# Third expert layer: the shared expert's eight tiles from normed rows on chip, with the routing interleaved

## The reference

```
gelu = lambda t: jax.nn.gelu(t, approximate=False)
shared = gelu(x @ W1s + b1s) @ W2s + b2s
rw = jax.nn.softmax(x @ Wr, axis=-1)
topw, topi = jax.lax.top_k(rw, 2)
topw = topw / jnp.sum(topw, axis=-1, keepdims=True)
mask = jnp.sum(jax.nn.one_hot(topi, 8) * topw[..., None], axis=-2)
h = gelu(jnp.einsum('bsd,edf->bsef', x, W1p) + b1p)
priv = jnp.einsum('bsef,efd->bsed', h, W2p) + b2p
return shared + jnp.einsum('bsed,bse->bsd', priv, mask)
```

## Time and profile before

| | us |
|---|---|
| median of three runs | 1201.09 (1198.06 to 1204.16) |
| profiled execution | 1190.06 |
| its span, first to last instruction | 1188.3 |
| TensorE busy | 951.9 (80%) |
| VectorE busy | 737.2 (62%) |
| ScalarE busy | 504.8 (42%) |
| GpSimd busy | 468.1 (39%) |
| mean granted TensorE clock | 0.891 |

### The profile page before, as it was taken

How to read it: one execution, slowest core, us unless ns; L and a number is a source line. 1 busy time by engine, 2 the same in 40 slices (tenths; PEclk the granted TensorE clock), 3 DMA queues, 4 the chain that set the end, 5 groups by cost and what they waited for, 6 DMA issues and landing times. The chain is left out here.

```text
span 1188.3 us, 23797 instructions
## 1 busy us (share of the span) xinstructions
PE 951.9 (80%) x7426; PEld 885.7 (75%) x7426; DVE 737.2 (62%) x1699; ACT 504.8 (42%) x933; POOL 468.1 (39%) x480
## 2 busy tenths in 40 slices
PE   5784978528888859856995999999628995899993
PEld 1684878525888859855895999999625885899993
DVE  4586655475777757647555656665454786666664
ACT  2151656310555617631102777776413451343441
POOL 1052565211867626530132355554103452345441
PEclk9695999869879969997997999999859997899997
DMA  6005965410000053744124051119440003846853
GB/s 231 1 23 174 299 222 175 123 41 0 6 10 10 10 182 99 229 137 130 54 67 177 29 196 35 37 47 334 175 128 2 6 14 114 312 162 206 278 186 125
DMA packets 65388, 142.22 MB, mean 120 GB/s; under 512 B 11008, under 2 KB 42656, under 8 KB 60320
## 3 DMA queue, kind: packets, MB, share of 16 engines
q1 hardware_dynamic: 55520, 114.52, 28.3%
q0 software_dynamic: 9792, 26.75, 7.5%
HBM read 219.36 MB, written 18.61 MB: 200 GB/s over the span
## 5 line engine op out<-in xcount | busy, mean ns | idle before, releaser
L1602 PE MATMUL r_pH<-e_xsT,e_w 128*128 128x128 f32 x2560 | 309.0, 278 | 25.5 <-DMA e_w<-w_in 20.6
L1602 PEld LDWEIGHTS r_pH<-e_xsT,e_w 128*128 128x128 f32 x2560 | 298.4, 194 | 29.5 <-issue 22.5
L1551 POOL DMA_INDIRECT y_rows<-e_ys,e_to x102 | 166.5, 1632 | 259.6 <-DVE e_idx L1670 122.2
L1682 DVE TENSOR_TENSOR e_w_lo<-e_w,e_w_hi 128x1024 fp32r<-128x1024 f32 (+1 forms) x102 | 156.2, 1532 | 45.8 <-ACT e_w_hi L1638 45.1
L1615 PE MATMUL r_pY<-e_w_hi,e_h_hi 128*128 128x256 f32 x528 | 159.1, 301 | 7.4 <-issue 5.8
L1638 ACT ACTIVATE e_w_hi<-e_w 128x1024 fp32r<-128x1024 f32 (+1 forms) x102 | 132.3, 1297 | 70.3 <-DMA e_w<-w_in 70.2
L1687 DVE TENSOR_TENSOR e_h_lo<-xnT,e_h_hi 128x512 fp32r<-128x512 f32 (+1 forms) x102 | 86.6, 849 | 119.8 <-ACT e_h_hi L1654 119.8
L1615 PE MATMUL r_pY<-e_w_lo,e_h_hi 128*128 128x256 f32 x528 | 150.4, 285 | 0.0
L1615 PE MATMUL r_pY<-e_w_hi,e_h_lo 128*128 128x256 f32 x528 | 150.4, 285 | 0.0
L448 PE MATMUL g_o<-g_V,g_pT 128*128 128x65 f32 (+2 forms) x896 | 145.0, 319 | 4.8 <-ACT g_pT L407 4.8
L1650 ACT ACTIVATE xnT<-r_pH,e_w 128x128 f32<-128x128 f32 x416 | 115.5, 377 | 71.3 <-PE r_pH L1602 71.1
(11 more groups left out here) (275 smaller groups left out, 1412.9 us busy)
## 6 DMA issues: line engine op xcount, KB each, us to landing
e_w<-w_in SPq DMA_DIRECT2D x64, 1024.0 KB
e_w<-w_in SPq DMA_DIRECT2D x84, 512.0 KB
e_w<-w_in SPq DMA_DIRECT2D x32, 1028.0 KB
e_w<-w_in SPq DMA_DIRECT2D x52, 514.0 KB
e_b<-b_in SPq DMA_DIRECT2D x84, 128.0 KB
e_w<-y_rows SPq DMA_DIRECT2D x24, 256.0 KB, 5.0
p_adj<-adj_in SPq DMA_DIRECT2D x8, 512.0 KB, 7.4
xn_rows<-xn SPq DMA_DIRECT2D x32, 128.0 KB, 1.7
```

The lines of the kernel that those rows point to most:

```text
L1551: pool.indirect_dma_start(out=y_rows[:, :], in_=ys[b][:, :], in_offset=None, out_offset=bass.IndirectOffsetOnAxis(ap=to[b][:, :], axis=0))\
L1602: ins = nc.tensor.matmul(pH[b % 2][:, f, :], w1[b][:, at:at + P], xsT[b % 2][:, c, :], start=(c == 0), stop=(c == DC - 1))
L1682: nc.vector.tensor_tensor(w2_lo[b % 2][:, :], w2[b][:, :], w2_hi[b % 2][:, :].bitcast(F32), ALU.subtract).then_inc(w2_split, 1)
```

## The change

The shared expert's weights get buffers of their own for the whole kernel (w1_own, w2_own, b2_own) and are loaded during graph2, behind the second adjacency tile in SyncE's queue. A class OwnTiles computes the eight shared tiles ahead of the loop: `rise` reads the turned normed rows xnT directly, so that no rows are loaded, turned or copied; w2's rounding and remainder are made once; `end` adds the result to x at once, so that nothing of it goes through y_rows. The steps of `gate` are cut into parts that each engine issues between the steps of these tiles: TensorE counts ranks behind the first `rise` and makes the table of pairs behind the fourth `fall`; VectorE has slots at k = 0, tiles at 1, columns at 2, rows and destinations at 5; ScalarE its column at 2. Their results in PSUM move from pH to pT. The 72 matmuls of `rouse` go in this layer. The routed tiles are then tiles 0 to 21 of the loop, with HEAD = 2 turns written out; their slots' first guess is expert 0 and expert 4. The eighth shared `fall` and `end` are queued behind the first routed `rise`. `combine` loads and adds two rows. hT gets buffers of its own in this layer, since xnT stays in use. The other layers keep their order.

```diff
...
+        w1_own, w2_own = keep("w1_own", [P, DC * 1024 + 1024 // P]), keep("w2_own", [P, 1024 // P * D])
+        b2_own = keep("b2_own", [P, D])
         lg = keep("lg", [P, NT, 16])
...
+                            for buf, src in own_weights:
+                                sp.dma_start(buf, src).then_inc(own_loaded, 16)
                     front.store(sp)
...
+
+            def tensor_table(pe):
...
-                rouse(spare, 72)
-
-            def scalar_part(act):
+                if spare is not None:
+                    rouse(spare, 72)
...
+            links = []
+
+            def vector_onehots(dve):
+                links.append(linker(dve, vd))
+                link = links[0]
...
-                if shared:
-                    nc.vector.tensor_copy(dest[:, 0:first], own[:, 0:first])
-                    nc.vector.memset(etab[0:1, 0:first], E)
-
+
+            def vector_slots(dve):
+                link = links[0]
...
+            def vector_tiles(dve):
+                link = links[0]
...
+
+            def vector_columns(dve):
+                link = links[0]
...
+                nc.vector.tensor_scalar(etab[0:1, 0:R], et[:, :], float(E - 1), None, ALU.min)
+                nc.vector.tensor_scalar(more[:, :], turns[0:1, :], float(-HEAD), None, ALU.add).then_inc(tiles_known, 1)
+
+            def vector_rows(dve):
+                link = links[0]
...
-            K = 3 if shared else 2
...
+            K = 2
...
-                    if shared:
-                        link(nc.vector.tensor_tensor(acc, acc, yg[t][:, 2, :], ALU.add))
...
+        class OwnTiles:
...
+            def rise(self, pe, k):
+                F = self.FC * P
+                if k == 0:
+                    pe.wait_ge(self.loaded, 48)
+                if k >= 2:
+                    pe.wait_ge(self.ready, k - 1)
+                for f in range(self.FC):
+                    for c in range(DC):
+                        ins = nc.tensor.matmul(self.pH[k % 2][:, f, :], w1_own[:, c * F + f * P:c * F + (f + 1) * P],
+                                               xnT[:, c, k * P:(k + 1) * P], start=(c == 0), stop=(c == DC - 1))
+                ins.then_inc(self.risen, 1)
+            def fall(self, pe, k):
+                pe.wait_ge(self.w_split, 1)
+                pe.wait_ge(self.split, k + 1)
+                if k >= 2:
+                    pe.wait_ge(self.kept, k - 1)
+                m = k % 2
+                for f in range(self.FC):
+                    for n, (h, w) in enumerate(((self.h_hi, self.w2_hi), (self.h_hi, self.w2_lo), (self.h_lo, self.w2_hi))):
+                        ins = nc.tensor.matmul(self.pY[m][:, :], h[m][:, f, :], w[:, f * D:(f + 1) * D],
+                                               start=(f == 0 and n == 0), stop=(f == self.FC - 1 and n == 2))
+                ins.then_inc(self.fallen, 1)
+            def clear(self, pe, b):
+                if b == 1:
+                    pe.wait_ge(self.ready, NT)
+            def round_weights(self, act):
+                act.wait_ge(self.loaded, 48)
+                nc.scalar.activation(self.w2_hi[:, :], w2_own[:, :], ACT.Copy).then_inc(self.w_rounded, 1)
+            def activate(self, act, k):
+                F, m = self.FC * P, k % 2
+                act.wait_ge(self.risen, k + 1)
+                if k >= 2:
+                    act.wait_ge(self.split, k - 1)
+                    act.wait_ge(self.fallen, k - 1)
+                for f in range(self.FC):
+                    ins = nc.scalar.activation(self.hT[m][:, f, :], self.pH[m][:, f, :], self.function,
+                                               bias=w1_own[:, DC * F + f:DC * F + f + 1])
+                ins.then_inc(self.ready, 1)
+                act.wait_ge(self.ready, k + 1)
+                nc.scalar.activation(self.h_hi[m][:, :, :], self.hT[m], ACT.Copy).then_inc(self.rounded, 1)
+            def split_weights(self, dve):
+                dve.wait_ge(self.w_rounded, 1)
+                nc.vector.tensor_tensor(self.w2_lo[:, :], w2_own[:, :], self.w2_hi[:, :].bitcast(F32), ALU.subtract)\
+                    .then_inc(self.w_split, 1)
+            def split_hidden(self, dve, k):
+                m = k % 2
+                dve.wait_ge(self.rounded, k + 1)
+                nc.vector.tensor_tensor(self.h_lo[m][:, :, :], self.hT[m], self.h_hi[m][:, :, :].bitcast(F32), ALU.subtract)\
+                    .then_inc(self.split, 1)
+            def end(self, dve, k):
+                m = k % 2
+                dve.wait_ge(self.fallen, k + 1)
+                nc.vector.tensor_tensor(self.ys[m][:, :], self.pY[m][:, :], b2_own[:, :], ALU.add).then_inc(self.kept, 1)
+                dve.wait_ge(self.kept, k + 1)
+                nc.vector.tensor_tensor(x[:, k, :], x[:, k, :], self.ys[m][:, :], ALU.add)
...
-                hT = [xnT[:, n, 0:F].rearrange("p (f q) -> p f q", q=P) for n in range(2)]
+                if own_loaded:
+                    hT = [ph.sb(f"hT{n}", [P, FC, P])[:, :, :] for n in range(2)]
+                else:
+                    hT = [xnT[:, n, 0:F].rearrange("p (f q) -> p f q", q=P) for n in range(2)]
...
-                        return E if shared else b * E // UN
+                        return b * E // UN
...
-                        if isinstance(i, int) and t < first:
-                            if not early(i, b, UN):
-                                pool.wait_ge(turned, t - UN + 1)
-                            pool.dma_start(xs[b][:, :], xn_rows[t * P:(t + 1) * P, :]).then_inc(xs_loaded[b], 16)
-                            return
                         if not early(i, b, UN):
                             pool.wait_ge(turned, t - UN + 1)
-                        pool.wait_ge(idx_ready, t - first + 1)
+                        pool.wait_ge(idx_ready, t + 1)
                         pool.nop(nofuse=True)
...
+                        if own and early(i, b, UN):
+                            pe.wait_ge(own.kept, NT - 1 + b)
...
                     def step(i, b):
                         turn(i, b)
+                        if own and early(i, b, UN):
+                            own.clear(pe, b)
                         if not early(i, b, 1):
                             rise(*before(i, b, 1))
+                        if own and early(i, b, 2) and b == 1:
+                            own.fall(pe, NT - 1)
                         if not early(i, b, 2):
                             fall(*before(i, b, 2))
-                    gate_tensor(pe)
+                    ranks, table_of_pairs = gate_tensor
+                    if own:
+                        for k in range(NT):
+                            own.rise(pe, k)
+                            if k == 0:
+                                ranks(pe)
+                            if k > 0:
+                                own.fall(pe, k - 1)
+                            if k == 4:
+                                table_of_pairs(pe)
+                    else:
+                        ranks(pe)
+                        table_of_pairs(pe)
                     last = loop(pe, step)
                     rise(last, UN - 1)
                     fall(last, UN - 2)
...
+                        if own and early(i, b, UN):
+                            act.wait_ge(own.fallen, NT - 1 + b)
+                            act.wait_ge(own.split, NT - 1 + b)
...
-                    gate_scalar(act)
+                    exps, column = gate_scalar
+                    exps(act)
+                    if own:
+                        own.round_weights(act)
+                        for k in range(NT):
+                            own.activate(act, k)
+                            if k == 2:
+                                column(act)
+                    else:
+                        column(act)
...
-                        if not early(i, b, first - UN):
-                            next_rows(b, t + UN - first)
+                        next_rows(b, t + UN)
...
+                        if own and early(i, b, 2) and b == 1:
+                            own.end(dve, NT - 1)
...
-                    gate_vector(dve)
-                    dve.wait_ge(rows_known, 1)
-                    if not shared:
+
+                    def first_rows(dve):
+                        dve.wait_ge(rows_known, 1)
                         for b in range(UN):
                             next_rows(b, b)
-                    gate_dest(dve)
+                    onehots, slots, tiles, columns, rows, destinations = gate_vector
+                    onehots(dve)
+                    if own:
+                        for k in range(NT):
+                            for part in {0: [slots, own.split_weights], 1: [tiles], 2: [columns],
+                                         5: [rows, first_rows, destinations]}.get(k, []):
+                                part(dve)
+                            own.split_hidden(dve, k)
+                            if k > 0:
```

(6 more changed lines are left out.)

## The result

The changed kernel takes 1181.01 us, the median of four runs (1178.82 to 1184.53); the kernel before, timed beside it, takes 1199.80 (1198.06 to 1204.16). The ratio is 0.9849, with a 95% interval of 0.9819 to 0.9879, or 18.1 us less. The profiled execution took 1179.99 us, 10.1 less than that of before, at a mean granted clock of 0.894. So the change makes the kernel faster, by a little more than the forecast 15.3 us; the forecast time was 1185.8 us, and the measured 1181.01 lies at the lower edge of its own range, 1181 to 1192. In three later comparisons, each on a chip of its own, the kernel before took 1190.69 to 1191.55 us, so only ratios and savings are compared across comparisons.

What follows compares the result with a forecast made beforehand. Routing was taken as bound by VectorE's chain, the tiles by TensorE; 10.1 us saved at the layer's start plus 5.2 at its end, 15.3 off the median 1201.09, gives 1185.8 us, own range 1181 to 1192, all cases 1178 to 1196.

Steps and rivals of the forecast that it cites:

- First product and slow clock: At the layer's start, first product 3.49 us plus 1.7 lost to the low clock, bounds 0 and 3.5.
- Ranks: TensorE's rank matmuls, placed behind the first own product at the layer's start, would take 1.3 us.
- Stall before the first second product: TensorE would wait 1.5 us for VectorE's slots and two splits before tile 0's product 2, bounds 0 and 3.
- No wait between: Routing pieces between shared tiles stay hidden, 1.7 us of slack left; rival that they are not covered: about 1194, chance 0.12.
- Handover: From shared to routed tiles, first routed product 3.9 us after the seventh second product, a stall of 3.5.
- the loop's count: VectorE's reading of the count before copying the turned routed rows, taken as 0.7 us, bounds 0.2 and 1.5.
- To the first routed product: From the third expert layer's start to its first routed product, 57.7 us against 69.0, 11.3 saved.
- Clock at the handover: A clock fall after the wait before the first routed product, charged 1.2 us, bounds 0 and 3.
- End of the layer: Combining two rows instead of three cuts 19.62 us after the last add to 14.45: 5.2 saved, bounds 4 and 6.
- Own weights: Their 2.2 MB of loads in SyncE's queue of the graph stage would cost 0, bounds 0 and 2.
- GpSimd beside VectorE: Six slot comparisons, 3.57 us, beside VectorE's split of the weights, would cost nothing.
- The rival price: GpSimd comparisons of 0.6 us before each split make the first second product's stall 2.7 us, time 1187.0; no chance given.

Runs made afterwards that it cites:

- e6: Changed kernel with a third row per tile loaded and added into an unread buffer when combining: 1181.60 us, ratio 0.9911 to the kernel before.
- e9: Changed kernel with no edit, timed again: 1174.92 us against 1191.15 for the kernel before, ratio 0.9874.
- e3: Changed kernel with the first two routed tiles turned before the last own first product and copied earlier: 1171.72 us, ratio 0.9835 to the kernel before.
- e5: Changed kernel with routing pieces slots, tiles and columns all ahead of VectorE's split of the own weights: 1185.65 us, ratio 0.9939 to the kernel before.
- e4: Changed kernel with 42 idle-filling matmuls around the last steps of graph2, before the layer's entry: 1173.27 us, ratio 0.9831 to the kernel before.
- e7: Changed kernel with both the early turns and copies and the 42 filling matmuls before the layer's entry: 1169.65 us, ratio 0.9797 to the kernel before.
- e1: Changed kernel with the routing and its 72 filling matmuls back in one piece ahead of the shared tiles: 1189.22 us, ratio 0.9993 to the kernel before.
- e10: Early turns and copies plus 42 filling matmuls on the changed kernel, run again beside the unedited changed kernel: 1167.27 us, ratio 0.9805 to the kernel before.
- e2: Kernel before with two rows combined, the shared expert's row neither loaded nor added (output incomplete): 1188.77 us, ratio 0.9987 to the kernel before.

## Why the prediction was right

The forecast saved 15.3 us. The layer's distances, each the mean of the two profiles of a kernel, give 244.3 - 229.1 = 15.2, and the two timings 18.1 and 15.0. That the layer agrees to 0.1 us is partly luck: the start gave 11.2 (11.3 forecast), the end 4.1 instead of 5.2, and the 1.2 charged for a fall of the clock at the handover weren't paid in either profile of the changed kernel, so that two mis-sized terms cancel. The forecast time of 1185.8 started from the 1201.09 of the first timing, and is 4.8 us too high: 1.3 by the kernel before, whose median came out at 1199.80 beside the changed one, and the rest by the saving. The steps, in the prediction's order:

- **First product and slow clock: undersized.** I gave the low clock 1.7 us. From its start to the ranks it took 5.81, so 2.3 were lost; it took 5.1 in e6, 6.2 in e9, 6.3 in e3 and 6.5 in e5, a loss of 1.6 to 3.0, and with the fillers 3.6 (e4, e7). The low stretch that I took for the price, lasted 3.4 us; here the clock was low in all of the first 3 us and about half of the next. The bound of 3.5 held.
- **Ranks 1.1 (1.3 forecast), table 0.5 (0.7).** Both a little cheaper.
- **Stall before the first second product: 1.5, as forecast.** The order of events, ranks, slots, two splits, was the forecast one: the second product came 6.14 us after the first product's end instead of 6.3. The forecast counts from start to start (1.11 for the ranks, 3.49 for the product, then 1.54 of stall); the 1.21 in the row's bracket is shorter because the last matmul's modelled end, 3.82 after the product's start, lies later.
- **No wait between.** VectorE's pieces stay under TensorE's work as worked out, and e5 shows the other case: with the pieces in one lump 9.4 us come back. The 1.7 us of slack in the prediction are those of the hidden rows' way to the second product; what a piece has to fit in is VectorE's idle time of a tile, 4.42 us.
- **Handover: 2.86 of idle time (3.5), the mechanism shown by e3.** From the end of the seventh second product, 687.39, the first routed product came after 3.47 us, not 3.9. The oversized term is the loop's count, which no row had priced: VectorE's idle time before the copy is 0.24 us, and 0.7 was assumed. (That the 0.24 us are the reading of the count is argued from the program's order; the row names no releaser.)
- **To the first routed product: 57.7 forecast, 57.66 measured, 58.03 again.** The exact agreement is partly luck: the clock's 0.6 us and some 0.1 of small differences too few, and the handover's 0.4 and the small steps' 0.4 too many, cancel.
- **Clock at the handover: 1.2 charged, the mechanism real but not certain.** Six profiles hold this wait of 2.85 to 2.87 us. In four (e1, e4, e5, e6) the next product took 5.44 us, in two (after, e9) 3.81. A fall costs 1.63, four in six are 1.1 on average. That the bounds went down to 0 was right, that the likeliest case was a fall fits the six, but the changed kernel's own two profiles don't show one. What decides between the two outcomes stays open.
- **End of the layer: 5.2 charged, 4.1 measured**, 18.9 to 14.8 in means. The layer with two rows had nearly the right price for after (14.45), but the single profile of before, 19.62, stood high; the second had 18.22.
- **Own weights: 0, as forecast.** SyncE's queue in the changed kernel:

```profile
553.47 0.94 SPq L938 DMA_DIRECT2D w_own<-w_in  x2
...
558.15 40.96 SPq L933 DMA_DIRECT2D g_adjT<-adjT_in  x5
```

The own loads lie in a gap of the queue and delay nothing in it: the third adjacency tile is issued 12.64 us after the graph stage's first load (545.51), where it was issued after 12.63 before (555.51 in the earlier trace rows, from 542.88). From that first load to the layer's entry it took 87.7 and 88.9 us in the two profiles of the changed kernel, for 87.3 and 88.8 before.
- **GpSimd beside VectorE.** The rival price, by the Trainium skill's page "SBUF — State Buffer", section "SBUF: two separate sides", was a stall of 2.7 us; it was 1.5. The row that was to speak for no cost is read a little wrong in the prediction: from 633.59 to 636.82 VectorE has 16 steps and not 18, 0.20 us each; the argument stays. The six comparisons in the changed kernel, by tile (columns: least, median and longest duration in ns, then first and last start), and behind them the same of e5:

```profile
L1266 POOL TENSOR_SCALAR r_on_slot<-iota_row,r_slot_f x6: 596/622/3716, 641.7 to 648.0; 128x128 bf16<-128x128 f32 x6
```

```profile
L1266 POOL TENSOR_SCALAR r_on_slot<-iota_row,r_slot_f x6: 594/610/631, 638.3 to 641.2; 128x128 bf16<-128x128 f32 x6
```

One comparison took 3716 ns and the others some 0.6 us each. VectorE's split had begun at 641.62, GpSimd's first comparison at 641.74, and it ended at 645.46, when both splits were over; the splits kept their 2.28 and 1.22 us. The first comparison took 3717 to 3719 ns in e3, e4, e6, e7, e9 and e10 too. In e5 the comparisons met only routing steps of 0.15 to 0.63 us, and none was long. That agrees with the rule of this page of the Trainium skill that the one that starts first blocks the other for its whole length; my application of it was wrong, since VectorE was first. GpSimd's 3.3 us cost nothing, as the table of pairs is due 19 us later.

What carried the prediction was the chain of events at the two places where engines hand over to each other, with a duration for each from a row. What it did not hold was the price of one start at the low clock.

**Left open.** Why e1 gained only 0.8 us in its timing (at most 3.6) with a layer 5 us shorter, and whether e2's longer waits for weights are its own. These are the two kernels that keep the gain of the end alone, and neither timing shows it in full; the start's gain is better borne out, by e5 and e1 against the changed kernel. The timing of the changed kernel in its first comparison, 18.1 us, is 2.9 above the layer's 15.2, with 15.2 inside its interval (14.5 to 21.7) and inside the second one's.

## What to carry to other kernels

Where an engine that sets the pace waits for a chain of small steps on another, look for work that doesn't depend on the chain, and deal the chain out in pieces shorter than that engine's idle time in one tile (here 3.4 and 4.2 us of routing in 4.4 us of idle VectorE): in one lump it gave back more than half of the layer's gain (e5). After such a change look at the seams, since each is a chain of its own: turning the next kind of tile one tile earlier and keeping the clock up across the stage's start brought another 5.2 to 5.6 us of the start (e7, e10). Price a stage by its own distance between two events in several profiles, because the rest of this kernel, which the change hardly touches, varied by 10 us over the twelve profiles.

## What the hardware showed that was not expected

- **The same wait, two outcomes.** 2.86 us of idle time on TensorE were followed by 32 matmuls in 3.81 us or in 5.44, in 2 and 4 profiles. The two are both profiles of the changed kernel, but e6, one of the four, runs the same program up to that point. The cause is open. A start of the layer after the sparse steps of graph2 cost 1.6 to 3.0 us in five profiles (after, e3, e5, e6, e9), and 42 small matmuls that nobody uses took nearly all of that away (e4, e7, e10).
- **VectorE's next instruction went first.** GpSimd's comparison, waiting since 0.12 us after VectorE's first split had begun, did not get in between that split and the next, and took 3716 instead of about 600 ns, and nearly the same in six more profiles.
- **The loop's head**, where VectorE reads its count, shows as 0.24 us of idle time on VectorE.
